# Two chunks' front half interleaved ahead of the loop, bias rows applied by VectorE, one packed table tile, and written-out last steps

## What is computed

```python
# block 0: down 256 -> 64, relu, up 64 -> 256
w_down = down_project * dg[:, None, :] + db[:, None, :]   # dg, db, ug, ub: conditions @ gamma or beta
down = einsum('bsd,bdh->bsh', x, w_down)
w_up = up_project * ug[:, None, :] + ub[:, None, :]
x = x + einsum('bsh,bhd->bsd', relu(down), w_up) + x
# block 1: x += x @ (U[:, :-1] @ V) + U[:, -1] @ V,  U = (mu @ W_dec + b_dec) as [257, 30]
# block 2: modulated linear (style, demod) to kx = q = k = v, 16 heads of 16;
#          scores over the heads of one token, softmax, weighted sum, second modulated linear
# block 3: layer norms of x with gathered gains and shifts (250 pathways, 5 compartments, 5 steps,
#          3 scales), three small networks of the conditions, six parts of 256 concatenated,
#          out = LN(silu(cat @ W1 + b1) @ W2 + b2); x += out
```

## Time and profile before

| | |
|---|---|
| median of 3 runs | 552.02 us (549.22 to 572.51) |
| the profiled execution | 556.02 us |
| its span in the profile | 554.2 us, 9364 instructions |
| PE busy | 467.3 us, 84% |
| DVE, ACT, POOL busy | 344.7, 290.2, 171.7 us |
| chain that ended last, by engine | PE 62%, DVE 15%, ACT 6%, DMA 6% |

### The profile page before, as it was taken

One profiled execution on the slowest core, in us unless ns is written; L12 is line 12 of the kernel. 1 busy time (PEld: TensorE's weight loads), 2 busy tenths in 40 slices (PEclk: granted clock), 3 DMA queues, 4 the chain that ended last, 5 costly groups with the idle time before them and its releaser, 6 DMA issues.

```text
span 554.2 us, 9364 instructions
## 1 busy us (share of the span) xinstructions
PE 467.3 (84%) x3768; PEld 260.9 (47%) x3768; DVE 344.7 (62%) x641; ACT 290.2 (52%) x433; POOL 171.7 (31%) x146
## 2 busy tenths in 40 slices
PE   4895576734799999999999999999999879878682
PEld 3673244421365555456554655554565435333241
DVE  0374655862386598479749865984797369333813
ACT  0102586372556696678397647966783876100010
POOL 3009993200323132331422231223314233511301
PEclk9998879966699999999999999999999989967796
DMA  5991600606326432904372265328043621402001
GB/s 153 348 248 53 178 2 20 164 23 148 93 80 173 133 116 69 259 25 151 90 215 77 80 154 152 115 71 237 6 153 75 192 77 44 114 1 76 0 1 38
DMA packets 68736, 61.00 MB, mean 110 GB/s; under 512 B 53910, under 2 KB 55572, under 8 KB 68308
## 3 DMA queue, kind: packets, MB, share of 16 engines
q1 hardware_dynamic: 64404, 43.86, 29.1%
q0 software_dynamic: 3712, 12.59, 7.0%
q10 hardware_dynamic: 576, 3.95, 2.0%
HBM read 39.18 MB, written 21.07 MB: 109 GB/s over the span
## 4 chain that ended last, share of the span: by engine, by line
PE 62%; DVE 15%; ACT 6%; DMA 6%; issue 4%; SPq 4%; POOL 1%; ACTq 0%; POOLq 0%; DVEq 0%
PE ph L592 15%; PE pk L571 8%; PE ph L554 6%; PE ph L680 5%; PE pp L554 4%; ACT bd L808 3%; PE pp L713 2%; PE pp L601 2%; PE pp L696 2%; PE pp L652 2%; DMA k_dram<-kxb 2%; PE pp L728 2%; PE ph L674 2%; DMA kt<-k_dram 2%; DVE kx L1204 1%
## 5 line engine op out<-in xcount | busy, mean ns | idle before, releaser
L808 ACT ACTIVATE bd<-kc,ownrow 128x512 f32<-128x512 f32 x128 | 80.7, 709 | 0.3
L821 ACT ACTIVATE bd<-vc,ownrow 128x512 f32<-128x512 f32 x128 | 80.7, 710 | 0.0
L396 POOL TENSOR_TENSOR demod<-demod,neghalf 128x32 f32<-128x32 f32 x8 | 43.5, 5453 | 36.2 <-DVE demod L978 36.2
L554 PE MATMUL ph<-attnT,owT 128*128 128x512 f32 x64 | 36.4, 723 | 9.1 <-DVE h L1128 4.9
L434 POOL TENSOR_TENSOR attnT<-attnT,style 128x1024 f32<-128x1024 f32 x8 | 15.8, 1972 | 89.9 <-DMA attnT<-av_dram 89.9
L571 PE MATMUL pk<-bd,kc 128*32 128x128 f32 x1024 | 35.6, 298 | 5.0 <-ACT bd L808 5.0
L571 PEld LDWEIGHTS pk<-bd,kc 128*32 128x32 f32 x1024 | 30.4, 120 | 19.6 <-issue 9.8
L592 PE MATMUL ph<-tT,w 128*128 128x512 f32 x64 | 31.1, 631 | 2.1 <-DVE tT L1077 2.1
L554 PE MATMUL pp<-ys,kwT 128*128 128x512 f32 x64 | 30.7, 625 | 2.6 <-DVE ys L1187 2.6
L680 PE MATMUL ph<-w,hid 128*128 128x256 f32 x96 | 31.4, 455 | 0.0
L571 PE MATMUL pk<-bd,et 128*32 128x128 f32 x1024 | 31.1, 273 | 0.0
(11 more groups left out here) (200 smaller groups left out, 947.8 us busy)
## 6 DMA issues: line engine op xcount, KB each, us to landing
xin<-in_x SPq DMA_DIRECT2D x8, 512.0 KB, 4.8
x_dram<-x SPq DMA_DIRECT2D x8, 512.0 KB, 2.6
k_dram<-kxb SPq DMA_DIRECT2D x16, 256.0 KB, 3.4
kt<-k_dram SPq DMA_DIRECT2D x8, 512.0 KB
v_dram<-kxb SPq DMA_DIRECT2D x8, 512.0 KB
vt<-v_dram SPq DMA_DIRECT2D x8, 512.0 KB, 6.1
x1r<-x_dram SPq DMA_DIRECT2D x8, 512.0 KB, 3.5
av_dram<-av SPq DMA_DIRECT2D x8, 512.0 KB, 5.8
```

The source lines that it names most:

```text
L396: gp.tensor_tensor(q, q, neghalf[:, 0:4 * CB].rearrange("p (l a b) -> p l a b", l=2, a=2), ALU.pow).then_inc(gs_dem, 1)
L554: ins = mm(dst[:, 512 * o:512 * o + 512], w[:, k, 128 * o:128 * o + 128], x[:, k, :], start=(k == 0), stop=(k == 1))
L808: fn(bd[:, h, :, 16 * b:16 * b + 16].rearrange("p (q z) x -> p q z x", z=2), kc[:, 16 * h:16 * h + 16, :].rearrange("p q (z x) -> p q z x" ...
L821: fn(bd[:, h, :, 16 * b:16 * b + 16], vc[:, SH * h:SH * h + SH, :], ACT.Copy, scale=ownrow[:, 1, b:b + 1]).then_inc(s, 1)
```

## The change

The computation stays the same. There are five parts.

**1. Opening.** Role a of chunks 0 and 1 and the setup move out of the steps into a written-out `opening()`, where the two chunks alternate; the loop starts at step 1 with chunk 0 in role v, and role a begins with chunk 2 at step 2. Chunk 1's second up product goes to bank `pk`, and its row-sum term is built in `attnT`. On SP the keys of chunk 1 are stored and read in step 1, the late loads stand behind the loads of layers and of chunk 1's input. Lines of PE's opening, cut:

```diff
+                first_factor(0)
+                first_factor(1)
...
+                mm(P0, w_up[:, D:D + 128], act0, start=True, stop=True).then_inc(p_up, 1)
+                first_factor(2)
+                after(pe, d_x, 1, 16)
+                after(pe, v_up, 0)
+                turn(P23, xin, p_xT)
+                first_factor(3)
...
+                demod_sums()
...
+                after(pe, v_ys, 0)
+                proj(P23, kwT, ys, p_kx)
+                after(pe, v_up, 1)
+                networks_hidden()
+                after(pe, v_x0, 1)
...
+                after(pe, v_ys, 1)
+                proj(P23, kwT, ys, p_kx)
+                networks_out()
```

**2. Row sums.** PE writes the sums on all 128 rows (P0) where 64 were written; the products with `db_rows` and `ub_rows` are gone; DVE multiplies the sums by `dbT` and `ubT`, which hold the same numbers with features on partitions. VectorE's lines:

```diff
                     after(ve_, p_down, a)
-                    tt(by_batch(row_in), by_batch(P0[64:128, :]), per_batch(batch_eye[64:128, :], 64, a), ALU.mult
-                       ).then_inc(v_row_in, 1)
+                    tt(by_batch(act0), by_batch(P0[64:128, :]), per_batch(dbT[64:128, :], 64, a), ALU.mult
+                       ).then_inc(v_bt, 1)
                     after(ve_, a_act0, a - 1)
                     tt(by_batch(t1), by_batch(P0[0:H0, :]), per_batch(dg[:, :], H0, a), ALU.mult).then_inc(v_t1, 1)
...
-                    after(ve_, p_db, a)
                     after(ve_, v_t1, a)
-                    tt(t1, t1, P1[0:H0, :], ALU.add).then_inc(v_t2, 1)
...
+                    after(ve_, v_bt, a)
+                    tt(t1, t1, act0, ALU.add).then_inc(v_t2, 1)
...
                 if a is not None:
                     after(ve_, p_up, a)
-                    tt(by_batch(row_mid), by_batch(P0[64:128, :]), per_batch(batch_eye[64:128, :], B, a), ALU.mult
-                       ).then_inc(v_row_mid, 1)
+                    tt(by_batch2(ys[:, :, :]), by_batch(P0).unsqueeze(1).to_broadcast([128, 2, CB, S]), per_batch2(ubT[:, :, :], a),
+                       ALU.mult).then_inc(v_us, 1)
                     tt(by_batch2(x0[:, :, :]), by_batch2(halves(P23)), per_batch2(ug[:, :, :], a), ALU.mult
                        ).then_inc(v_up, 1)
...
-                if a is not None:
-                    after(ve_, v_up, a)
-                    stt(x0[:, :, :], xT[:, :, :], 2.0, x0[:, :, :], ALU.mult, ALU.add).then_inc(v_x0a, 1)
...
+                if d is not None:
                     after(ve_, p_o, d)
                     tt(by_batch2(tmp_o[:, :, :]), by_batch2(halves(ph[:, :])), per_batch2(demod[:, 1, :, :], d), ALU.mult
                        ).then_inc(v_o, 1)
...
                 if a is not None:
-                    after(ve_, p_ub, a)
+                    after(ve_, v_up, a)
+                    stt(x0[:, :, :], xT[:, :, :], 2.0, x0[:, :, :], ALU.mult, ALU.add).then_inc(v_x0a, 1)
                     after(ve_, v_x0a, a)
-                    tt(x0[:, :, :], x0[:, :, :], halves(P01), ALU.add).then_inc(v_x0, 1)
+                    after(ve_, v_us, a)
+                    tt(x0[:, :, :], x0[:, :, :], ys[:, :, :], ALU.add).then_inc(v_x0, 1)
```

The matmuls that go, on PE:

```diff
-                if a is not None:
...
-                    mm(P1[0:H0, :], db_rows[64:128, :], row_in, start=True, stop=True).then_inc(p_db, 1)
...
-                if a is not None:
-                    after(pe, v_row_mid, a)
-                    for o in range(2):
-                        ins = mm(P01[:, 512 * o:512 * o + 512], ub_rows[64:128, 128 * o:128 * o + 128], row_mid, start=True, stop=True)
-                    ins.then_inc(p_ub, 1)
...
                                          x0[:, k, S * q:S * q + S], start=(z == 0 and k == 0), stop=(z == 1 and k == 1),
                                          skip_group_check=True)
                     ins.then_inc(p_u, 1)
-                if v is not None:
-                    after(pe, a_et0, v)
-                    after(pe, a_bv0, v, 8)
-                    values(0, p_av0)
```

```diff
                 for s in range(3):
-                    for src, dst in work:
-                        ordered(cp(dst[s], src))
-                    for src, dst in work:
-                        if s < 2:
-                            ordered(tt(src, src, dst[s], ALU.subtract))
+                    ordered(cp(parts[:, s, :], pack))
+                    if s < 2:
+                        ordered(tt(pack, pack, parts[:, s, :], ALU.subtract))
...
+                sp.dma_start(tab_dram[0:5], parts[0:5, :, :]).then_inc(s_vec, 16)
+                sp.dma_start(tab_dram[5:9], parts[32:36, :, :]).then_inc(s_vec, 16)
+                sp.dma_start(vec_dram, parts[64:128, :, 0:D]).then_inc(s_vec, 16)
+                sp.wait_ge(s_vec, 3 * 16)
...
+                sp.dma_start(tables[0:24, 0:3 * D], classes[:, 0:3 * D]).then_inc(s_tab, 16)
+                sp.dma_start(tables[0:24, 3 * D:].rearrange("p (c j) -> p c j", j=D),
+                             classes[:, 3 * D:4 * D].unsqueeze(1).to_broadcast([24, NC, D])).then_inc(s_tab, 16)
+                sp.dma_start(tables[32:56, 3 * D:].rearrange("p (c j) -> p c j", j=D),
+                             vec_dram.rearrange("(c b) s j -> (b s) c j", b=CB)).then_inc(s_tab, 16)
+                sp.dma_start(b2_parts[:, :].rearrange("p (z j) -> p z j", z=2),
+                             tab_dram[8, :, 0:D].unsqueeze(1).to_broadcast([3, 2, D])).then_inc(s_tab, 16)
...
+                    if first(v):
+                        after(sp, a_kxb, 1, 2)
+                        after(sp, d_kt, 0, 16)
+                        keys_out()
+                        after(sp, d_kw, 1, 32)
+                        after(sp, a_kc, 0, 2)
+                        keys_in()
+                        small_tables()
```

```diff
+                for b in range(b0, b1):
+                    ts(bd[:, h, :, 16 * b:16 * b + 16].rearrange("p (q z) x -> p q z x", z=2),
+                       kc[:, 16 * h:16 * h + 16, :].rearrange("p q (z x) -> p q z x", z=3)[:, :, 0:3:2, :],
+                       ownrow[:, 0, b:b + 1], None, ALU.mult).then_inc(s, 1)
...
+                hidden(2, tT, p_ht)
+                after(pe, v_hn, e, 4)
+                turn(P23, h1, p_hnT)
+                after(pe, v_sT, e)
+                hidden(10, xnT, p_hs)
+                after(pe, g_ao, d)
+                after(pe, a_hnT, d - 1)
+                proj(P23, owT, attnT, p_o)
+                after(pe, v_hT, e)
+                hidden(0, hnT, p_hid, stop=True)
...
+                ins.then_inc(p_x2k, 1)
+                after(pe, g_oh, d)
+                gain(P01, D, p_tg)
+                hidden(4, x2T, p_hx, start=True, bank=pk)
```

More of the change, by code:

```diff
@@ L362, in _ @@
+            for n in range(1, NC):
                 step(n, *roles(n))
+            step_v7(NC - 1, NC - 2)
+            step_d7(NC - 1)
             sp.wait_ge(d_out, 16 * NC)
@@ L461, in _ @@
+            for n in range(1, NC):
                 step(n, *roles(n))
+            step_v7(NC - 2, NC - 3)
+            step_d7(NC - 1, NC - 2)
+            step_e7(NC - 2, NC - 1)
         @block.tensor
@@ L729, in step @@
                     ins.then_inc(p_x2k, 1)
+                if v is not None:
+                    after(pe, a_et0, v)
+                    after(pe, a_bv0, v, 8)
+                    values(0, p_av0)
                 if a is not None:
-                    if first(a):
-                        pe.wait_ge(vs_u, 4)
                     after(pe, v_x0, a)
@@ L777, in _ @@
+            opening()
+            for n in range(1, NC):
                 step(n, *roles(n))
+            step_v7(NC - 1, NC - 2, NC - 3)
+            step_d7(NC - 1, NC - 2)
+            step_e7(NC - 2, NC - 1)
         @block.scalar
@@ L834, in outputs_back, with key_bias, opening @@
                    ACT.Copy).then_inc(s, 1)
+            def key_bias():
+                for f in range(2):
+                    fn(kxb[:, f, :], kx[:, f, :], ACT.Identity, bias=cols[:, 2 + f:3 + f]).then_inc(a_kxb, 1)
+            def opening():
+                after(act, p_xT, 0)
+                fn(xT[:, :, :], halves(P23), ACT.Copy).then_inc(a_xT, 1)
+                after(act, v_t2, 0)
+                fn(act0, t1, ACT.Relu).then_inc(a_act0, 1)
+                after(act, p_xT, 1)
+                after(act, v_x0a, 0)
+                fn(xT[:, :, :], halves(P23), ACT.Copy).then_inc(a_xT, 1)
+                after(act, v_t2, 1)
+                after(act, p_up, 0)
+                fn(act0, t1, ACT.Relu).then_inc(a_act0, 1)
             def step(n, a, v, d, e):
@@ L843, in step @@
                 if v is not None:
-                    after(act, v_kx, v)
-                    after(act, d_kw, v - 1, 32)
-                    after(act, d_vw, v - 1, 16)
-                    for f in range(2):
-                        fn(kxb[:, f, :], kx[:, f, :], ACT.Identity, bias=cols[:, 2 + f:3 + f]).then_inc(a_kxb, 1)
+                    if v != 1:
+                        after(act, v_kx, v)
+                        after(act, d_kw, v - 1, 32)
+                        after(act, d_vw, v - 1, 16)
+                        key_bias()
                     if first(v):
@@ L918, in _, with step_e7 @@
```

(10 more changed lines are left out.)

935 lines of the change are left out of this document (805 added, 130 removed).

## The result

The changed kernel is faster: over the runs of both its time is 0.936 of the kernel before, with an interval of 0.926 to 0.946. Its profiled execution took 515.35 us with a span of 513.6, where 554.2 stood before: -40.6, and the prediction had -49. Its four runs took 515.35, 515.34, 530.32 and 530.04 us (median 522.7), where 503 was predicted; the ratio times the 552.02 of before is 517.

A forecast was written before the change was run, and what follows sets the result against it. PE was taken to fill the middle, its shortening limited by hand-overs to DVE. Span 554.2 - 24 (opening) - 5 (full steps) - 20 (end) = 505.2, so 507 profiled and 503 against the median 552.02; range 490 to 524.

The forecast's parts named there:

- The full steps: Steps 3 to 7: 3.2 us leave PE per step, but only 1.1 a step gets through, -5 over five steps.
- The two waits: Full steps: PE waits about 1 us each ahead of the turn of x2T and the product with V.
- the addition of twice the input: Full steps: moved behind x2T, it lies in DVE's chain from the projection's end to u, costing 1.2 us.
- The opening: Up to step 3: step 3 begins at 142 instead of 165.5, -24 us; -15 with late loads, -29 if nothing is cold.
- Step 8: First of the last steps: end at 463.4 instead of 464.31, -1; up to 5 later if DVE's blocks take 1.09.
- Step 9: Last steps: nothing changes up to the turn of h1, 11.3 us; the step takes 30 us, -21.
- The prediction's own sign for this step, over 38: Step 9: the prediction counts as wrong if the step takes over 38 us.
- Step 10: From chunk 7's xn turn to the end: its 39 us stay, or fall to 35 with a full clock.
- B: Rival, opening and steps 8 to 10: half clock holds longer in the new stretches, +15, 518 us; chance 0.18.
- A: Rival, full steps: all of PE's shorter work gets through, 492 us; chance 0.12.
- C: Rival, opening: gain still waits for tables or late loads hold the networks; half or more lost, 515 to 530; chance 0.11.
- D: Rival, full steps: two new PE waits lower the clock, 12 us more per step, 563 us, slower than before; chance 0.02.

The follow-up runs named there:

- The filled runs: Changed kernel with unread products in TensorE's waits: span 510.7; with chunk 6's h in ys's space and fewer products, ratio 0.907; filled more closely, 0.8975.
- the row sums alone: Kernel before plus only the row-sum part (VectorE multiplies 128-row sums, products with db_rows and ub_rows gone): span 563.0, steps 3 to 7 50.03 in the mean.
- `attnT` later: Changed kernel with GpSimd's scaling of attnT in step 9 moved behind the one-hot tile: step 9 took 39.5 us, 2.2 longer.
- twice the input ahead of `tT`: Changed kernel with the addition of twice the input back ahead of tT: steps 3 to 7 took 50.24, 50.27, 51.87, 50.25 and 52.15 us.
- the table parts source by source: Changed kernel with table parts made by 15 operations, per source, instead of 5: PE's wait ahead of step 2's first turn 14.32 us, not 7.84.

## Why the prediction was right and where it was wrong

**The full steps** were right with their reason: 1.1 a step forecast, 1.17 measured, at 49.5. The two waits stand where it put them, at 0.88 and 0.40. Of the reason one sentence fell: that the addition of twice the input, moved behind `x2T`, lies in the chain and costs its 1.2. Moved back it costs 0.8 a step, and 2.4 where the clock falls. The chain is VectorE's from the statistics of y on, and the place behind `x2T` is where the addition does least harm.

**The opening** gave 18.9 for 24. The mechanism was right: kx at 49.3 and 62.4 (51 and 62), scores at 69.3 (68.2), the table parts done at 95.0 (92.9), the gain released by the shift, the tables off the path. The terms that failed are durations at half clock that the sum took at full clock, and one reading. The networks' product ahead of the first scores took 3.30 (1.94 where the clock was full), the second scores, which VectorE waited for, 1.7 more than at full clock, and step 2 began 2.2 late. The reading: from step 2's start to the last write of `av` 7.5 passed, not 6.2 (7.1 in the trace before). So the up product was 3.6 late and step 3 4.6 (146.6 for 142, both at the turn of the softmax weights). The filled runs show what the clock is worth here: with the waits filled the same list reached step 3 9.6 earlier. Unchanged code also reached it at 141.6, 144.8, 145.6 and 145.8 in four runs, so a forecast of this stretch has some 4 us of spread.

**Step 8** gave 2.7 for 1, and most of the surplus is luck. With the old list in the changed kernel it takes 44.4 and with the new one 43.5, so the new list gives 0.9; 1.7 is the projection, at full clock where the trace before had it slower. The twelve blocks take 0.48 each on VectorE (3.26 for eight in a row, 1.65 for four), near the lower end of what the prediction allowed.

**Step 9** is the step that failed: "Up to the turn of h1 nothing changes, 11.3 us". It took 17.2: 3.56 are the wait for the store of chunk 5, 1.5 the collision with GpSimd, and 0.8 is the net of the rest. Chunk 5's last operation, a wait for ScalarE's copy and `tT` now stand ahead of h, which could have started 4.3 us into the step and not at once; against that, the 3.38 of h's first operation fell to 1.22. Behind the turn 20.1 passed for the 18.7 forecast, with the turn and the next product at half clock after PE's wait of 9.1. The lists show that VectorE's last operation on the tile and its reuse now almost follow each other; the prediction costed the order of operations and put the tile's reader, the store, at nothing. With h in another tile the turn comes after 11.7 and the step takes 31 to 32, where 30 was forecast. The prediction's own sign for this step, over 38, was set too wide to show the miss: 37.3 was measured.

**Step 10** kept its 39; nothing of the 4 us that a full clock could give came. It took 37.2 to 37.4 once the wait in step 9 was 3.63 and not 9.10, and 35.6 with its last wait filled too, near the 35 named for a full clock.

**The rivals.** The span came 8.4 us above the forecast of 505.2. B (half clock longer in the new stretches) has a part in it, in the opening and behind the turn in step 9; the 5.1 of store and collision are in no rival. A did not happen, C neither. D did not happen in the changed kernel, and its mechanism was produced by an edit, at 1.6 to 1.9 us a step. With it falls the prediction's sentence that D needs far less activity than a full step has: in one of the steps in which the clock fell PE was busy for 48.9 of 51.9 us.

## What to carry to other kernels

When a list of operations is reordered, follow each tile to its last reader, transfers too: an operation moved next to the reuse of its tile turns a hidden store into a wait. A product taken off the busiest engine is worth what is left after the hand-overs that it covered: of 2.45 us of TensorE's work 0.66 came out. Where TensorE waits several microseconds on the way to the end, a filling product in a free bank is cheap, but its duration has to be measured first: 14 of them ran 12.3 us in a wait of 7.8, and behind a fill that ended 2.5 us early the clock fell again.

## What the runs showed of the hardware

- In some executions TensorE keeps the durations of half clock until some 50 us. Four traces have it: the row sums alone, `attnT` later, twice the input ahead of `tT`, and the table parts source by source. It is not one kind of instruction. In the changed kernel and in the run with `attnT` later, the opening's first up product and 60 of the 120 weight loads of `w_dec` (ns of one behind the comma):

```profile
26.89 1.98 PE L793 MATMUL pp<-mid,w_up 64*128 64x512 f32 x4
L664 PEld LDWEIGHTS ph<-xnT,bd 128*128 128x128 f32 x60 | 6.9, 192 | 0.0
```

```profile
33.02 3.78 PE L793 MATMUL pp<-mid,w_up 64*128 64x512 f32 x4
L664 PEld LDWEIGHTS ph<-xnT,bd 128*128 128x128 f32 x60 | 13.0, 333 | 0.0
```

- The granted clock in the profile can be wrong at the start. The first of the two windows is of the run with `attnT` later and shows 1.00, the second is of the row sums alone and shows 0.50; the up product takes 3.78 us and a load 333 ns in both:

```profile
24.00:36.00 12.00, 12.00 (x47) 10.32 (x47) 3.77 (x6) 0.00 (x0) 0.00 (x0) 1.00 1.06 254
```

```profile
24.00:36.00 12.00, 12.00 (x46) 10.26 (x47) 4.37 (x7) 0.63 (x1) 0.00 (x0) 0.50 1.06 239
```

  The changed kernel's own first turn, at 12.02, takes 1.91 where 1.04 is usual, under a granted clock of 1.00. Durations of like products tell the clock there, the column does not. Why it rises late in some executions stays open; nothing was tried on it.
- VectorE's scaling of 128x256 takes 0.40 to 0.41 us where GpSimd is idle for most of it and up to 2.54 beside GpSimd operations.
- In a full step a wait of 0.88 us left TensorE's clock at 1.00 in five steps of five; behind one of 1.92 it fell in two of five. Behind a wait of 3.63 us in step 9 it fell in one of two executions of the same code.
